# Graph and mixture layers on one core: experts of the third layer half a block later, one-hots ahead of evictions, a bank half for layer 0's root product

## The reference, cut to what matters

```python
def _rgcn_layer(x, W, root, bias, src, dst, seg):
    agg = segment_sum(x[src], seg, num_segments=N_REL * N_NODES)      # seg = edge_type * N_NODES + dst
    agg = agg.reshape(N_REL, N_NODES, -1)
    return einsum('rnd,rde->ne', agg, W) + x @ root + bias

def gnn(x):                                   # 6250 nodes of 256 features, 206250 edges, 8 relations
    h = relu(_rgcn_layer(x, W[0], ...)); h = relu(_rgcn_layer(h, W[1], ...))
    return sigmoid(_rgcn_layer(h, W[2], ...))

def mix(x):                                   # 8 heads of 32; softmaxes over 4 keys and over the nodes
    h = layernorm(x); xm = h @ Wx + bx
    q = softmax(xm @ Wq, -1); k = softmax(xm @ Wk, -2); v = xm @ Wv
    fx = (q @ (k.T @ v)) @ Wo + bo + x
    return gelu(layernorm(fx) @ W1 + b1) @ W2 + b2 + fx

def moe(tokens):                              # 8 experts, the best 2 of each token are weighted
    combine = top2_weights(softmax(tokens @ router_w.T))
    return tokens + sum(combine[:, e] * (gelu(tokens @ w1[e] + b1[e]) @ w2[e] + b2[e]) for e in range(8))

xn = layernorm(x)
x = x + gnn(xn) + mix(xn)
return x + moe(layernorm(x))
```

## Time and profile before

| | us |
|---|---|
| median of 3 timed runs | 6513.6 (6508.7 to 6524.8) |
| span of the profiled execution | 8038.5 |
| TensorE busy in it | 5658.1 (70%) |
| GpSimd busy | 4625.1 (58%) |
| VectorE busy | 2215.5 (28%) |
| ScalarE busy | 1034.0 (13%) |

### The profile page before, as it was taken

How to read it: one execution, slowest core, us unless ns; L and a number is a source line. 1 busy time by engine, 2 the same in 40 slices (tenths; PEclk the granted TensorE clock), 3 DMA queues, 4 the chain that set the end, 5 groups by cost and what they waited for, 6 DMA issues and landing times.

```text
span 8038.5 us, 86017 instructions
## 1 busy us (share of the span) xinstructions
PE 5658.1 (70%) x22890; PEld 4136.2 (51%) x22890; DVE 2215.5 (28%) x6194; ACT 1034.0 (13%) x2706; POOL 4625.1 (58%) x4920
## 2 busy tenths in 40 slices
PE   8946666666656677777777777766676666766667
PEld 3434444444444445555555555545565555555556
DVE  8711111111111122222222222213333333333333
ACT  2200000000001011111111111111111111111112
POOL 1166666666666656666666666655555555555554
PEclk9977887788778888888888888888888888888888
DMA  6633333333333344344444444443233333323332
GB/s 189 189 102 110 113 112 110 115 115 114 114 114 112 115 127 117 116 121 120 120 119 117 119 120 119 124 128 88 86 87 89 89 89 88 89 87 89 91 88 67
DMA packets 354391, 888.01 MB, mean 110 GB/s; under 512 B 86234, under 2 KB 179294, under 8 KB 335623
## 3 DMA queue, kind: packets, MB, share of 16 engines
q0 software_dynamic: 232080, 633.91, 26.9%
q10 hardware_dynamic: 114178, 243.16, 10.4%
q1 hardware_dynamic: 7740, 5.99, 0.2%
HBM read 697.11 MB, written 185.60 MB: 110 GB/s over the span
## 4 chain that ended last, share of the span: by engine, by line
PE 39%; another core or an unknown queue 32%; issue 15%; DVE 6%; ACT 4%; ACTq 2%; DVEq 1%; DMA 1%; POOL 0%; POOLq 0%; SPq 0%
PE ps_out L1434 16%; PE ps_y L1405 7%; PE ps_y L1699 4%; PE ps_b L1710 3%; PE ps_c L1710 2%; PE ps_tr L1614 2%; DVE r L1289 1%; DVE onehot L1022 1%; PE ps_b L1405 1%; PE ps_c L1405 1%; PE ps_c L1602 1%; ACT L810 1%; ACT L574 1%; PE ps_b L1602 1%
## 5 line engine op out<-in xcount | busy, mean ns | idle before, releaser
L517 POOL DMA_INDIRECT ring<-table,gather_idx x4836 | 4576.4, 946 | 3030.0 <-issue 1391.3
L1434 PE MATMUL ps_out<-ring,onehot 128*125 x8400 | 2148.6, 403 | 261.6 <-issue 221.5
L1434 PEld LDWEIGHTS ps_out<-ring,onehot 128*125 128x125 f32 x8400 | 1625.0, 200 | 653.8 <-issue 415.8
L1434 PE MATMUL ps_out<-ring,onehot_more 128*125 x2448 | 783.2, 476 | 832.0 <-DVE onehot_more L1022 596.0
L1405 PE MATMUL ps_y<-W,hT 128*125 128x512 f32 (+1 forms) x2400 | 1138.8, 615 | 170.9 <-issue 69.7
L1434 PEld LDWEIGHTS ps_out<-ring,onehot_more 128*125 128x125 f32 x2448 | 550.1, 236 | 1036.1 <-issue 937.8
L1405 PEld LDWEIGHTS ps_y<-W,hT 128*125 128x125 f32 x2400 | 496.2, 210 | 677.8 <-issue 552.1
L849 DVE COPY y_stage<-ps_y 125x512 f32<-125x512 f32 x150 | 103.6, 690 | 2174.5 <-remote 1231.6
L1022 DVE TENSOR_TENSOR onehot<-targets,ps_out 128x500 f32<-128x500 f32 x1050 | 647.2, 671 | 180.8 <-issue 138.8
L1022 DVE TENSOR_TENSOR onehot_more<-targets,ps_out 128x250 f32<-128x250 f32 x612 | 239.8, 414 | 1016.2 <-remote 416.7
L533 ACT COPY y_stage<-ps_y 125x512 f32<-125x512 f32 x350 | 201.1, 587 | 2455.3 <-PE ps_y L1405 1165.7
(11 more groups left out here) (193 smaller groups left out, 3643.0 us busy)
## 6 DMA issues: line engine op xcount, KB each, us to landing
table<-y_stage ACTq DMA_DIRECT2D x147, 896.0 KB
ring<-table,gather_idx POOLq DMA_INDIRECT x4836
table<-y_stage ACTq DMA_DIRECT2D x147, 104.0 KB
xn_in<-xn_scratch ACTq DMA_DIRECT2D x100, 125.0 KB
base<-y_stage ACTq DMA_DIRECT2D x100, 125.0 KB
base_in<-base ACTq DMA_DIRECT2D x100, 125.0 KB
x_in<-in_x_dram ACTq DMA_DIRECT2D x75, 125.0 KB
xn_scratch<-xn_in ACTq DMA_DIRECT2D x50, 125.0 KB
```

The costliest lines, as they stand in the source:

```text
L517: nc.gpsimd.indirect_dma_start(ring[0:n, c * D:(c + 1) * D], None, table[l], bass.IndirectOffsetOnAxis(ap=gather_idx[0:n, tile:tile + 1].b ...
L1434: return nc.tensor.matmul(ps_out[w % 2][0:WIN, 0:D], lhsT, ring[:, bass.ds(slot + j * D, D)], start=first, stop=last)
```

## The change

In layer 2, experts are spread over two windows: parts 2 to 5 of block w-2 stand behind units 0, 1, 3 and 4 of window w, parts 0 and 1 of block w-1 behind units 5 and 6, and the tokens' transposes move behind unit 3. ScalarE and VectorE follow: GELUs 4 to 7 of the old block surround tanh and the copy of the transposes, GELUs 0 to 3 of the new one come last; VectorE sums experts 0 to 3 and the bias of the old block ahead of `layer_out`, and experts 4 to 7 behind unit 6's one-hots, ahead of the new block's router. `warm` is left only in window 0. The tail runs both blocks. In layers 0 and 1 VectorE issues the one-hots of units 3 to 6 ahead of both evictions. In layer 0 block 4 goes to the free half of `ps_tr`, beside the transposes, and directly behind block 0.

```diff
@@ -360,7 +360,8 @@
         ORDERS = [(1, 0, 2, 3)] + [(1, 0, 4, 2, 3)] * 2
-        BANK = [(ps_y[0], ps_y[1], ps_b, ps_c)] + [(ps_y[0], ps_y[1], ps_y[0], ps_y[1], ps_y[1])] * 2
+        BANK = [(ps_y[0], ps_y[1], ps_b, ps_c)] + [(ps_y[0], ps_y[1], ps_y[0], ps_y[1], fifth)
+                                                   for fifth in (ps_tr[:, D:2 * D], ps_y[1])]
@@ -779,15 +780,25 @@
                 act.dma_start(xn_in[parity][:, :], rows(res_dram, w)).then_inc(xn_loaded[parity], 16)
-                if w == 0 or w >= 2:
+                old = window(w - 2) if w >= 2 else None
+                if w == 0:
                     warm(ACT.Exp)
                 if prev:
-                    squash(prev)
-                    copy_hT(3, prev)
-                    logits_exp(prev)
-                    gelus3(prev, range(E))
-                    if w < NW - 1:
-                        store_out(prev)
+                    both_blocks(old, prev)
...
+            def both_blocks(old, win):
...
+                if old:
+                    gelus3(old, range(4, 6))
+                squash(win)
+                if old:
+                    gelus3(old, range(6, E - 1))
+                copy_hT(3, win)
+                if old:
+                    gelus3(old, range(E - 1, E))
+                    store_out(old)
+                logits_exp(win)
+                gelus3(win, range(0, 4))
@@ -819,18 +830,9 @@
-            def experts(win):
-                logits_exp(win)
-                gelus3(win, range(E))
-                store_out(win)
...
             def phase3_tail(win):
-                warm(ACT.Exp)
-                squash(win)
-                copy_hT(3, win)
-                logits_exp(win)
-                store_out(window(win[0] - 1))
-                gelus3(win, range(E))
+                both_blocks(window(win[0] - 1), win)
+                gelus3(win, range(4, E))
                 store_out(win)
@@ -1109,12 +1111,9 @@
                 w = cur[0]
-                step(3, 4, 5)
+                step(3, 4, 5, 6)
                 if prev:
-                    evac_y(1, prev, 1)
-                step(6)
-                if prev:
-                    evac_y(1, prev, 4)
+                    evac_y(1, prev)
                 if w < NW - 1:
@@ -1175,12 +1174,9 @@
                 w, parity, turn = cur
-                step(3, 4, 5)
+                step(3, 4, 5, 6)
                 if prev:
-                    evac_y(2, prev, 1)
-                step(6)
-                if prev:
-                    evac_y(2, prev, 4)
+                    evac_y(2, prev)
                 if w < NW - 1:
@@ -1234,6 +1230,7 @@
                 dve.wait_ge(xn_loaded[parity], turn * 16 + (16 + 2 * 16 * (NW // 2)))
+                dve.wait_ge(tr_done, 2 * NW + w)
@@ -1301,23 +1298,27 @@
             def phase3(cur, prev, step):
-                step(3)
+                old = window(cur[0] - 2) if cur[0] >= 2 else None
+                step(3, 4, 5)
                 if prev:
-                    assert layer_out(prev) == P3_CHAIN
-                step(4, 5)
+                    both_blocks(old, prev)
+                step(6)
                 if prev:
-                    largest_logit(prev)
-                    router(prev)
-                    take(prev, range(0, 4))
-                    take_b2(prev)
-                step(6)
-                if prev and cur[0] < NW - 1:
-                    take(prev, range(4, E))
...
-            def whole_block(win):
+                    later_half(old, prev)
...
+            def both_blocks(old, win):
...
+                if old:
+                    take(old, range(0, 4))
+                    take_b2(old)
+                assert layer_out(win) == P3_CHAIN
...
+            def later_half(old, win):
...
+                if old:
+                    take(old, range(4, E))
                 largest_logit(win)
                 router(win)
-                sums(win)
@@ -1325,9 +1326,10 @@
             def phase3_tail(win):
-                assert layer_out(win) == P3_CHAIN
-                take(window(win[0] - 1), range(4, E))
-                whole_block(win)
+                old = window(win[0] - 1)
+                both_blocks(old, win)
+                later_half(old, win)
+                sums(win)
             layer(2, phase3, phase3_tail)
@@ -1373,6 +1375,8 @@
                 pe.wait_ge(hT_ready, T)
+                if phase == 1 or phase == 2 and win[0] == 0:
+                    pe.wait_ge(y_evac_dve, dve_blocks_before(phase, win[0]))
                 for k in range(K):
@@ -1394,10 +1398,10 @@
                         pe.wait_ge(y_evac_act, T * 3 + 1)
-                    if phase and b == 4:
+                    if phase == 2 and b == 4:
                         pe.wait_ge(y_evac_dve, dve_blocks_before(phase, w) + 1)
                     if phase and b == 3:
-                        pe.wait_ge(y_evac_dve, dve_blocks_before(phase, w) + 2)
+                        pe.wait_ge(y_evac_dve, dve_blocks_before(phase, w) + phase)
                     if phase == 0 and w == 0:
@@ -1511,15 +1515,13 @@
                 if prev:
-                    products(1, prev, (1, 0))
+                    products(1, prev, (1, 0, 4))
                 if w < NW - 1:
...
                     nc.tensor.matmul(ps_out[w % 2][0:WIN, 0:D], xnT[:, k, :], root0[:, k, :], start=False, stop=False)
-                if prev:
-                    products(1, prev, (4,))
                 if w < NW - 1:
@@ -1692,7 +1694,7 @@
-                    if e >= 2:
+                    if w * E + e >= 2:
                         pe.wait_ge(act_done, w * E + (e - 1))
@@ -1750,23 +1752,31 @@
-            PARTS_BEHIND = {3: (0,), 4: (1, 2), 5: (3, 4), 6: (5,)}
...
             def phase3(cur, prev, unit):
                 w = cur[0]
+                old = window(w - 2) if w >= 2 else None
                 for i in range(STATIC):
...
                     unit(i)
-                    if prev and i == 2:
-                        tokens_transposed(prev)
-                    if prev:
-                        for part in PARTS_BEHIND.get(i, ()):
-                            experts(prev, part)
+                    both_blocks(old, prev, i)
...
+            OLD_BEHIND = {0: 2, 1: 3, 3: 4, 4: 5}
+            NEW_BEHIND = {5: 0, 6: 1}
...
+            def both_blocks(old, win, i):
...
+                if win and i == 3:
+                    tokens_transposed(win)
+                if old and i in OLD_BEHIND:
+                    experts(old, OLD_BEHIND[i])
+                if win and i in NEW_BEHIND:
+                    experts(win, NEW_BEHIND[i])
             def phase3_tail(win):
-                tokens_transposed(win)
-                for part in range(6):
+                for i in range(STATIC):
+                    both_blocks(window(win[0] - 1), win, i)
+                for part in range(2, 6):
                     experts(win, part)
...
```

## The result

The changed kernel takes 6534.6 us against 6513.6 us (medians of seven executions each; the table of before calls the same seven "3 timed runs"), a ratio of 1.0032 with an interval of 1.0022 to 1.0042: **slower by 0.3%**. The 21.0 us are just over the 19.5 us that the prediction drew as the line between "no change" and "slower". The forecast was 6525.6. One of the seven executions took 9407 us at a mean granted clock of 0.67; the ratio leaves it out, and without it the median would be 6534.4.

What follows compares the result with a forecast made beforehand. Gather issue was taken to bound all three layers, summing to 6493 to 6509 us against 6513.6 measured. Layers and steady windows cost nothing; the tail's +7.4 and +4.6 make +12.0, so 6525.6 us, range 6507 to 6540.

Steps and rivals of the forecast that it cites:

- The bound: All three layers: gathers issued 1.25 us apart bind the timed runs, 2015 us a layer; ring-slot waits 0.3% at most.
- Rival (1): Layer 2: faster, since the profile's waits are real in the timed runs and evened work pays; 6359 us, chance 0.07.
- Layer 1's block 4: Layer 1: block 4 newly waits 2.6 us a window for block 1's eviction; free under gathers, 130 us without cover.
- Rival (2): Layer 1: slower, block 4's wait takes TensorE's window to 40.5 us, past GpSimd's 40.3; up to 6656 us, chance 0.10.
- The steady windows of layer 2: Third layer: expert 0's GELU about 5 us late, TensorE with 4.3 us to spare; costs nothing, 250 us without cover.
- The tail: After the last unit 6: half a block of experts more, uncovered; +7.4 to the transposes and +4.6 after, +12.0 us.
- the last term: Tail, from the last block's transposes to its expert 0 down product: 9.8 us, before 5.15, so +4.6.
- five cases: The forecast, no effect at all (together 0.78), faster (0.07), slower by layer 1 (0.10), a dearer tail (0.05).
- rival (3): Tail: 20 to 30 us dearer as VectorE and ScalarE interleave worse; 6534 to 6544 us, chance 0.05.
- the upper bound of the tail, 16.1: Tail: extra products 9.65 us, down 0, up 2 and up 3 2.65, three table loads 3.84; 16.1 us at most.
- tanh amid GELUs: Layer 2, ScalarE: tanh between GELUs costs between nothing and two loads of 1.28 us a window, hidden in steady state.
- What would show it: Signs: gathers 1.25 us apart, end 12 us longer than 29.5, transposes 14 us after unit 6, block 4 2 to 3 late.

Runs made afterwards that it cites:

- e4: The kernel before, with no edit, profiled once more; 6512.6 us timed, profiled span 6510.4 us.
- e2: Only the changes of layers 0 and 1 made to the kernel before, third layer left as before; 6514.1 us, ratio 1.0000.
- e1: Only the third layer's reordering made to the kernel before, layers 0 and 1 left as before; 6536.9 us, ratio 1.0034.
- e11: The changed kernel with all gathers, largest logit ahead of sums and one-hots, output store behind the new block's first GELUs; 6528.1 us, ratio 1.0025.
- e12: The changed kernel with every other gather left out, early logit and late output store, layers 0 and 1 as before the change; 5251.2 us, ratio 0.8059.
- e8: The kernel before with every other gather left out, matrix products kept; 5371.2 us, ratio 0.825.

## Why the prediction was right, and where it was not

*The bound: right.* Gathers 1.25 us apart in every layer make 2015.1, 2022.5 and 2017.9 us of the changed kernel, as the sum had it (2015 each). That the waits of the shown profile were that execution's alone, which the prediction could only argue, e4 shows: the same kernel without them. Rival (1) falls with it.

*Layer 1's block 4: right in mechanism and size.* TensorE and VectorE in a window of the changed kernel's layer 1:

```profile
4163.06 1.10 PE L1409 MATMUL ps_y<-W,hT 128*125 128x256 f32 x4 [2.47 <-DVE y_stage L851]
```

```profile
4159.88 2.43 DVE L1024 TENSOR_TENSOR onehot<-targets,ps_out 128x500 f32<-128x500 f32 x4 [0.76 <-issue]
4162.23 0.68 DVE L851 COPY y_stage<-ps_y 125x512 f32<-125x512 f32 x1
```

Predicted 2.6 us, here 2.5 (2.3 in the mean of the layer); free under the cover (e2), and 148 us without it where 130 were predicted. TensorE's busy time in the layer rises by 35 us with it (1620.8 to 1655.9, granted clock 0.98 to 0.97), which the price of 2.6 a window left out. Rival (2) needed a window over 40.3 us; with half the gathers it is 37.2.

*The steady windows of layer 2: the wait right, the room wrong.* "4.3 us to spare even at the recorded clock" divided busy time by windows and left the new wait out of the engine's own pace. That wait has a second cause, which the prediction put at nothing: the output store, "neither is waited for within 40 us", stands on ScalarE ahead of the exponential and waits for the old block's last sums, as the largest logit does on VectorE. Without its cover the wait is 5.0 us a window, 251.3 in all, as the prediction's "5 x 50 = 250" had it; the layer is 140 us longer by it than before, 267 longer than with the exponential early. But the layer's own pace is 39.4 to 40.0 us against gathers of 40.3: 0.3 to 0.9 us of room. The forecast of no cost was right by luck of a few tenths.

*The tail: right in mechanism, 7 us too small.* Predicted +12.0, measured +18.7. By its terms: from unit 6 to block 48's down 0, 1.8 predicted, 5.6 measured; from there to the weights' transpose 5.3 and 7.0; from there to the last block's transposes 7.0 and 7.3; from there to its down 0 9.8 and 11.6. The step that failed is **"its products to 1.8; down 0, up 2, up 3 of block 48 to 4.4"**: it took block 48's GELUs as ready, although in the prediction's own steady windows the same chain, sums, logit, table, exponential, table, makes them about 5 us late. VectorE and ScalarE of the changed kernel show it:

```profile
6482.80 1.00 DVE L1286 SCALAR_TENSOR_TENSOR r<-ps_b,combine,r 125x256 f32<-125x256 f32 x2
6483.83 1.00 DVE L1286 SCALAR_TENSOR_TENSOR r<-ps_c,combine,r 125x256 f32<-125x256 f32 x2
6484.87 0.17 DVE L1253 TENSOR_REDUCE small<-ps_a 125x1 f32<-125x8 f32 x1
```

```profile
6484.87 0.28 ACTq L831 DMA_DIRECT2D out_dram<-r  x1
6485.17 1.28 ACT L810 ACT_TABLE_LOAD   x1 [13.66 <-DVE r L1286]
6486.47 0.27 ACT L810 ACTIVATE probs<-ps_a,small 125x8 f32<-125x8 f32 x1
...
6488.14 1.13 ACT L821 ACTIVATE gT<-ps_y,vectors 128x125 f32<-128x125 f32 x4
```

The largest logit and the output store (L831) both come at 6484.87, when the sums are done, 1.5 us after unit 6 has started, and the GELU 3.3 us later. That is 3.8 of the 7.6 us by which the changed tail, 49.1, is longer than the worked-out 29.5 + 12.0 = 41.5 (the tail of before takes back some 0.8 of it, 30.3 in e4 for 29.5). The other term is the clock, read from the products' lengths: behind the wait two ups take 3.27 us instead of 1.95 (6515.72 in the same trace), a down behind the transposes 1.91 instead of 1.03; these are the most of the 1.7 and 1.8 us missed in the second and the last term.

How the two share the excess differs from execution to execution. e1 has no such wait (down 0 stands 3.6 us behind the start of unit 6) and is as long, by slower products. From the last unit 6 to the last block's down 0 the same 114 products keep TensorE busy 21.3 us in the changed kernel at a granted clock of 0.89, 23.3 in e1 at 0.79, 22.2 in e11 at 0.82 and 19.3 in e12 at 0.93. Nor does every wait slow what follows: behind the last block's 2.96 us down 0 takes 1.10 us in the changed kernel and 2.04 in e1.

e12 supports the first terms: with GELUs ready and the clock up, down 0 stands 1.8 us behind unit 6, the weights' transpose 5.3 behind that, the last transposes 7.3 behind that (1.8, 5.3 and 7.0 predicted). Its whole tail is 41.3 us against 29.5 of e8, 11.9 more where 12.0 were predicted, but that agreement is in part luck. The last term is 9.3 us where 9.8 were priced for a logit behind the sums, and here the logit is early while the down behind the transposes is as slow as in the changed kernel:

```profile
5224.05 1.91 PE L1721 MATMUL ps_b<-big,gT 128*125 128x256 f32 x4
```

So of the five cases it was rival (3), the dearer tail of 20 to 30 us, that came in size, at its lower edge (6534 to 6544, chance 0.05), and for its reason: VectorE and ScalarE interleave worse than the sum had them. The forecast came in kind. The range of 6507 to 6540 held the time only because it reached into that rival; the upper bound of the tail, 16.1, lay under the measured 18.7, because it counted work and loads, and no product at the lower clock. It also counted three down products (2.6 us) that stand behind the last unit 6 before the change too (6482.67 and 6483.53 in the rows of e4); without them it would have been 13.5.

*tanh amid GELUs: no load of its own.* ScalarE in a steady window of the changed kernel:

```profile
6462.55 0.62 ACT L821 ACTIVATE gT<-ps_y,vectors 128x125 f32<-128x125 f32 x2 [2.37 <-PE ps_y L1701]
6463.06 0.41 ACT L806 ACTIVATE h_sum<-h_sum 125x256 f32<-125x256 f32 x1
6465.12 0.62 ACT L821 ACTIVATE gT<-ps_y,vectors 128x125 f32<-128x125 f32 x2 [1.65 <-PE ps_y L1701]
```

The tanh (L806) runs between two GELUs, and a window has two loads, for the exponential and back. The Trainium skill (ScalarE: Activation LUTs, Table sets: the hidden batching unit) lists GELU's set without tanh; the measurement differs and decides. Of the prediction's two bounds for it, nothing and two loads, nothing was right.

*What would show it.* Gathers 1.25 us apart, block 4 2 to 3 us late: both seen. "The end some 12 us longer" and "transposes 14 us after it": seen in kind, 18.7 and 19.9 in size.

## What to carry to other kernels

Sum the queue that can't be hurried (its instructions times their pitch, and the edges) before any wait is read, and hold it against the timed runs: where it fills them, order within the steady state is free as long as no other engine's chain, waits included, passes that pace, and what is left open when that queue ends is the whole price. A software pipeline stage more pays its extra depth in the tail; if it is wanted, catch up while there are covered windows left, since one window is too late. And find an engine's room by opening the cover in an experiment, or by its chain with waits in it, not by its busy time.

## What was not expected

A gather of 32 rows costs nearly what one of 128 does: 870 and 871 ns in the mean against 946 to 948, with the same 0.305 us between two; most of the cost is the instruction's, not the rows'. The same kernel was profiled at 8038.5 and at 6510.4 us, with 886.2 us of waits for unnamed releasers in the one and none in the other. And the same half block, with two instructions moved in each window (the largest logit on VectorE, the output store on ScalarE), turned a loss of 140 us into a gain of 127 in the layer without its cover; 100 of these 267 us are TensorE's own busy time, 1686 against 1586, for the same products at another granted clock.
